# Queries packed two heads to a slot: four slot products per batch in place of six

## The reference, cut to what matters

```python
q = split_heads(tokens @ Wq, HEADS)
kv = split_heads(tokens @ Wkv, HEADS)
k, v = (kv[..., :DK], kv[..., DK:])
q, k, v = (l2norm(q), l2norm(k), l2norm(v))
sim = jnp.einsum('bhid,bhjd->bhij', q, k)
attn = jnp.square(jax.nn.relu(sim))
out = jnp.einsum('bhij,bhjd->bhid', attn, v)
out = tanh_norm(out)
```

## Time and profile before

| | |
|---|---|
| median of 3 runs | 542.15 us (540.87 to 542.36) |
| time of the profiled execution | 541.96 us |
| its span, first to last instruction | 539.8 us |
| outside the span | 2.2 us |
| mean granted clock of TensorE | 0.994 of full speed |
| busy: PE, DVE, ACT, POOL | 96%, 77%, 69%, 65% of the span |

### The profile page before, as it was taken

One profiled execution on the slowest core, in us unless ns is written; L12 is line 12 of the kernel. 1 busy time (PEld: TensorE's weight loads), 2 busy tenths in 40 slices (PEclk: granted clock), 3 DMA queues, 4 the chain that ended last, 5 costly groups with the idle time before them and its releaser, 6 DMA issues.

```text
span 539.8 us, 10360 instructions
## 1 busy us (share of the span) xinstructions
PE 519.2 (96%) x3334; PEld 389.9 (72%) x3334; DVE 417.8 (77%) x1001; ACT 370.3 (69%) x675; POOL 349.7 (65%) x311
## 2 busy tenths in 40 slices
PE   8798999999999999999999999999999999999997
PEld 7566667676766666778787777777778767788884
DVE  6767888889888886688588688598598678786765
ACT  6597878879788965454757945955955955855553
POOL 6756869696977782776568456466566555666562
PEclk9799999999999999999999999999999999999999
DMA  8400000101010001910762921940940850861930
GB/s 219 132 1 2 1 15 18 46 2 46 2 46 14 4 2 64 215 41 5 181 134 77 214 56 43 211 95 27 222 98 18 213 136 6 191 141 54 215 70 19
DMA packets 37269, 44.50 MB, mean 82 GB/s; under 512 B 5856, under 2 KB 20448, under 8 KB 37216
## 3 DMA queue, kind: packets, MB, share of 16 engines
q1 hardware_dynamic: 32528, 42.14, 33.7%
q10 hardware_dynamic: 4688, 1.71, 1.3%
HBM read 40.68 MB, written 3.15 MB: 81 GB/s over the span
## 4 chain that ended last, share of the span: by engine, by line
PE 45%; POOL 30%; issue 18%; DVE 5%; ACT 2%; POOLq 0%; DVEq 0%; ACTq 0%
PE PS L1317 44%; POOL hl L564 14%; POOL vi L458 4%; POOL sr L479 4%; POOL v L475 1%; POOL qs L467 1%; POOL rstd L504 1%; POOL sqq L469 1%; DVE aT L973 1%; POOL mrstd L555 1%; POOL rsA L443 1%; DVE n L944 1%; DVE PS L1186 0%; DVE hb L1191 0%; ACT sqv L612 0%
## 5 line engine op out<-in xcount | busy, mean ns | idle before, releaser
L564 POOL TENSOR_TENSOR hl<-hb,hh 128x512 fp32r<-128x512 f32 x127 | 164.6, 1297 | 128.7 <-ACT hh L792 127.8
L785 ACT ACTIVATE sil<-PS 128x512 f32<-128x512 f32 (+1 forms) x136 | 81.1, 596 | 78.2 <-PE PS L1317 73.1
L1186 DVE TENSOR_TENSOR PS<-sil,PS 128x512 f32<-128x512 f32 x128 | 88.3, 690 | 53.1 <-PE PS L1317 30.7
L1317 PE MATMUL PS<-fxh,wfh 128*128 128x512 f32 x264 | 104.6, 396 | 2.3 <-DVE hb L1191 1.5
L792 ACT ACTIVATE hh<-hb 128x512 fp32r<-128x512 f32 x128 | 80.4, 628 | 38.4 <-DVE hb L1191 37.4
L1317 PE MATMUL PS<-fxh,wfl 128*128 128x512 f32 x264 | 104.2, 395 | 0.0
L1317 PE MATMUL PS<-fxl,wfh 128*128 128x512 f32 x264 | 104.0, 394 | 0.0
L1191 DVE TENSOR_TENSOR hb<-PS,wbc 128x512 f32<-128x512 f32 x128 | 88.5, 691 | 12.3 <-issue 5.4
L973 DVE SCALAR_TENSOR_TENSOR aT<-PS,rl 128x1024 f32<-128x1024 f32 x64 | 75.8, 1218 | 20.3 <-ACT rl L627 20.2
L627 ACT ACTIVATE rl<-PS 128x1024 f32<-128x1024 f32 x64 | 63.8, 1028 | 19.0 <-PE PS L1317 18.9
L1317 PE MATMUL PS<-aT,v 128*64 128x256 f32 x512 | 62.3, 385 | 0.0
(11 more groups left out here) (197 smaller groups left out, 890.1 us busy)
## 6 DMA issues: line engine op xcount, KB each, us to landing
wbc<-w_dram SPq DMA_DIRECT2D x48, 512.0 KB, 11.8
wbc<-w_dram SPq DMA_DIRECT2D x32, 128.0 KB, 3.0
wbc<-w_dram SPq DMA_DIRECT2D x16, 256.0 KB, 4.3
wfs<-wf_dram SPq DMA_DIRECT2D x32, 98.0 KB, 2.1
band_dram<-zero SPq DMA_DIRECT2D x16, 80.0 KB, 1.7
band<-band_dram ACTq DMA_DIRECT2D x4, 320.0 KB, 2.9
Osb<-wa_dram SPq DMA_DIRECT2D x3, 256.0 KB, 3.6
X<-x_dram SPq DMA_DIRECT2D x1, 768.0 KB, 6.7
```

What stands on the lines that cost most here:

```text
L564: g.tensor_tensor(hl[:, n % RING, :], hb[:, n % RING, :], hh[:, n % RING, :].bitcast(F32), ALU.subtract).then_inc(F("hl"), 1)
L785: s.activation(sil[0:rows, n % 2, :], PS[0:rows, G0 + n % 2, :], ACT.Silu).then_inc(F("silu"), 1)
L1186: v_.tensor_tensor(PS[:, bank, :], sil[:, n % 2, :], PS[:, bank, :], ALU.mult).then_inc(F("t"), 1)
L1317: return nc.tensor.matmul(o, w, m, start=start, stop=stop)
```

## The change

The queries are packed like the keys: groups 0 and 1 share a block of 128 weight columns, groups 2 and 3 another. `queries(n)` makes both blocks in one bank with two slot products, `keys(n)` the keys with two more. ACT then reads the bank of the queries twice, each time through `Identity` with a scale that is a column of 0s and 1s per partition (`own`) and a bias that is a column of zeros: the first copy keeps the even groups' rows and sets the others to 0, the second the odd groups'. The bank counts as read only after the second copy; a semaphore `even` marks the first. `own` is made on DVE at the start by four small instructions. The weights are 256 columns fewer, and each group has one turn of a bank less (two per batch for queries and keys in place of three).

```diff
-WQ_G, WK_G = (0, 1, 4, 5), (2, 3)
-W_V = 2 * NQ * P
+EVEN, KEYS, ODD = 0, 1, 2
+W_Q, W_K, W_V = 0, 2 * P, 4 * P
-FIRST_WEIGHTS = (("in_wv0", slice(W_V, W_V + 512)), ("in_wv1", slice(W_V + 512, WA)), ("in_wq0", slice(0, 4 * P)),
-                 ("in_wq1", slice(4 * P, W_V)))
+FIRST_WEIGHTS = (("in_wv0", slice(W_V, W_V + 512)), ("in_wv1", slice(W_V + 512, WA)), ("in_wk", slice(W_K, W_V)),
+                 ("in_wq", slice(W_Q, W_K)))
...
-    order += [("v", 0, t, k) for t in range(2) for k in range(2)] + [("g", 0, j) for j in range(NQ)]
+    order += [("v", 0, t, k) for t in range(2) for k in range(2)] + [("k", 0), ("q", 0)]
...
-        order += coming(n, ("g", n, 0), ("g", n, 2), ("g", n, 1)) + [("nb", n)]
+        order += coming(n, ("q", n), ("k", n)) + [("nb", n)]
...
             def square_queries(n, k):
-                pool.wait_ge(*freed("g", n, 2 * k))
+                pool.wait_ge(*freed("q", n))
                 pool.wait_ge(*full("nb", n - 1))
-                g.tensor_tensor(qs[:, k, :], qk[:, n % 2, 2 * k, 0:L], qk[:, n % 2, 2 * k, L:2 * L], ALU.add).then_inc(A("qs"), 1)
+                g.tensor_tensor(qs[:, k, :], qk[:, n % 2, EVEN, k * L:(k + 1) * L], qk[:, n % 2, ODD, k * L:(k + 1) * L],
+                                ALU.add).then_inc(A("qs"), 1)
...
-            def keep_group(n, j):
-                act.wait_ge(*full("g", n, j))
+            def keep_queries(n, par):
+                act.wait_ge(*full("q", n))
+                if n == 0:
+                    act.wait_ge(cs("own"), 2)
+                    act.wait_ge(cs("zero"), 1)
                 after(act, A("S"), 2 * NG * (n - 1))
-                s.activation(qk[:, n % 2, j, :], PS[:, bank_of("g", n, j), :], ACT.Copy).then_inc(free_of("g", n, j), 1)
+                done = free_of("q", n) if par else A("even")
+                s.activation(qk[:, n % 2, (EVEN, ODD)[par], :], PS[:, bank_of("q", n), :], ACT.Identity, bias=zero[:, 0:1],
+                             scale=own[:, par:par + 1]).then_inc(done, 1)
+
+            def keep_keys(n):
+                act.wait_ge(*full("k", n))
+                after(act, A("S"), 2 * NG * (n - 1))
+                s.activation(qk[:, n % 2, KEYS, :], PS[:, bank_of("k", n), :], ACT.Copy).then_inc(free_of("k", n), 1)
...
-            keep_group(0, 0)
-            keep_group(0, 1)
+            keep_keys(0)
+            keep_queries(0, 0)
             square_values(0, 1)
-            keep_group(0, 2)
+            keep_queries(0, 1)
             relu(0)
...
                 relu_half(NG * b + 1, 0)
                 if more:
-                    keep_group(n, 0)
+                    keep_queries(n, 0)
                 relu_half(NG * b + 1, 1)
...
                 if more:
-                    keep_group(n, 2)
-                    keep_group(n, 1)
+                    keep_queries(n, 1)
+                    keep_keys(n)
                     square_keys(n)
...
             v_.tensor_copy(rowg[:, :], rowh[:, :]).then_inc(cs("rg"), 1)
+            v_.tensor_scalar(rowp[:, :], rowid[:, :], DK, None, ALU.bitwise_and).then_inc(cs("rp"), 1)
+            dve.wait_ge(cs("rp"), 1)
+            v_.tensor_copy(rowq[:, :], rowp[:, :]).then_inc(cs("rq"), 1)
+            dve.wait_ge(cs("rq"), 1)
+            for par in range(2):
+                v_.tensor_scalar(own[:, par:par + 1], rowq[:, 0:1], float(DK * par), None, ALU.is_equal).then_inc(cs("own"), 1)
...
             def first_square_queries(k):
-                dve.wait_ge(*freed("g", 0, 2 * k))
+                dve.wait_ge(*freed("q", 0))
...
-            def group(n, j):
-                bank, done = turn("g", n, j)
+            def slot_wise(n, w0, bank):
                 for part in range(2):
-                    cols = slice((2 * j + part) * P, (2 * j + part + 1) * P)
-                    last = split3(PS[:, bank, part * L:(part + 1) * L], wah[:, cols], wal[:, cols],
-                                  xTh[:, :], xTl[:, :])
-                last.then_inc(done, 1)
+                    cols = slice(w0 + part * P, w0 + (part + 1) * P)
+                    last = split3(PS[:, bank, part * L:(part + 1) * L], wah[:, cols], wal[:, cols], xTh[:, :], xTl[:, :])
+                return last
+
+            def queries(n):
+                bank, done = turn("q", n)
+                slot_wise(n, W_Q, bank).then_inc(done, 1)
+
+            def keys(n):
+                bank, done = turn("k", n)
+                slot_wise(n, W_K, bank).then_inc(done, 1)
+
+            def wait_queries(b, g):
+                if g % 2:
+                    pe.wait_ge(*freed("q", b))
+                else:
+                    pe.wait_ge(A("even"), b + 1)
...
             def score(i):
...
-                jq, q0, k0 = WQ_G[g] // 2, WQ_G[g] % 2 * L, g // 2 * L
-                pe.wait_ge(*freed("g", b, jq))
-                pe.wait_ge(*freed("g", b, 1))
+                jq, c0 = (EVEN, ODD)[g % 2], g // 2 * L
+                wait_queries(b, g)
+                pe.wait_ge(*freed("k", b))
...
                 if more:
                     pe.wait_ge(*freed("xT", n))
-                    for j in (0, 2, 1):
-                        group(n, j)
+                    queries(n)
+                    keys(n)
```

More of the change, by code:

```diff
@@ L183, in hybrid_layer @@
         rowg = sb("rowg", [P, 1])
+        rowp = sb("rowp", [P, 1], I32)
+        rowq = sb("rowq", [P, 1])
+        own = sb("own", [P, 2])
         sel = sb("sel", [P, 2, P], F32R)
@@ L226, in hybrid_layer @@
         Z = Sems(ctx, nc, "full0 full5 full6 full7 free0 free5 free6 free7")
-        ld = Sems(ctx, nc, "in_x0 in_x in_wv0 in_wv1 in_wq0 in_wq1 in_x1 in_wo in_wf0 in_wf1 in_wf2 in_wf3 in_wf4 in_wf5 in_wf6 in_wf7 in_sd in_gw in_wb in_bb zeroed")
-        cs = Sems(ctx, nc, "id0 id half floors rid ind0 indp0 ind indp rm rf rh rg sel fpad zero sel1 sdz wah wal wph wpl wfh wfl sdh sdl")
-        A = Sems(ctx, nc, "stats mv ve rstd xn xTh vraw sqv n2v nv n2o nbo qs sqq sqk rr vi vc0 vc vp S relu a av Oc sqO "
+        ld = Sems(ctx, nc, "in_x0 in_x in_wv0 in_wv1 in_wk in_wq in_x1 in_wo in_wf0 in_wf1 in_wf2 in_wf3 in_wf4 in_wf5 in_wf6 in_wf7 in_sd in_gw in_wb in_bb zeroed")
+        cs = Sems(ctx, nc, "id0 id half floors rid ind0 indp0 ind indp rm rf rh rg rp rq own sel fpad zero sel1 sdz wah wal wph wpl wfh wfl sdh sdl")
+        A = Sems(ctx, nc, "stats mv ve rstd xn xTh vraw sqv n2v nv n2o nbo even qs sqq sqk rr vi vc0 vc vp S relu a av Oc sqO "
                           "sr sr_half n th nmx rec f1 ff fhi f")
@@ L598, in tokens_high @@
                 if n:
-                    act.wait_ge(*full("g", n - 1, NQ - 1))
+                    act.wait_ge(*full("k", n - 1))
                 s.activation(xTh[:, :], PS[:, bank_of("xT", n), 0:L], ACT.Copy).then_inc(A("xTh"), 1)
@@ L612, in square_values @@
                 s.activation(sqv[:, :], v[:, n % 2, t, :], ACT.Square).then_inc(A("sqv"), 1)
[L614 to L617 removed]
+            def keep_queries(n, par):
[3 more added lines that the diff above has]
+                    act.wait_ge(cs("zero"), 1)
+                after(act, A("S"), 2 * NG * (n - 1))
+                done = free_of("q", n) if par else A("even")
[5 more added lines that the diff above has]
+                s.activation(qk[:, n % 2, KEYS, :], PS[:, bank_of("k", n), :], ACT.Copy).then_inc(free_of("k", n), 1)
             def square_keys(n):
[L620 removed]
+                act.wait_ge(*freed("k", n))
                 act.wait_ge(*full("nb", n - 1))
[L622 removed]
+                s.activation(sqk[:, :], qk[:, n % 2, KEYS, :], ACT.Square).then_inc(A("sqk"), 1)
             def relu_half(i, f):
@@ L1366, in score @@
                         rows = slice(SLOT * s, SLOT * (s + 1))
-                        last = mm(PS[:, S0 + s, jt * L:(jt + 1) * L], qk[rows, b % 2, 1, k0 + jt * P:k0 + (jt + 1) * P],
-                                  qk[rows, b % 2, jq, q0:q0 + L], True, True)
+                        last = mm(PS[:, S0 + s, jt * L:(jt + 1) * L], qk[rows, b % 2, KEYS, c0 + jt * P:c0 + (jt + 1) * P],
+                                  qk[rows, b % 2, jq, c0:c0 + L], True, True)
                         if jt == 1 and s % 2 == 1:
@@ L1497, in _ @@
             pe.wait_ge(cs("wpl"), 1)
-            group(0, 0)
-            group(0, 1)
+            keys(0)
             pe.wait_ge(cs("wpl"), 2)
-            group(0, 2)
+            queries(0)
             fill_idle(4, "xT", 1)
@@ L1514, in _ @@
                 if b < 2:
-                    fill_idle(4 if b == 0 else 8, "g", n, 0)
+                    fill_idle(4 if b == 0 else 8, "q", n)
                 if b == 0:
```

14 lines of the change are left out of this document (7 added, 7 removed).

## The result

The kernel with the packed queries takes 551.74 us in the median of 6 runs (549.13 to 554.53), the kernel before 542.07 in the 6 runs beside it: a ratio of 1.0189, 95% interval 1.0153 to 1.0226, slower by 9.7 us. Forecast were 549.8 and a range of 546 to 555. The profiled execution takes 552.22 us, with a span of 550.4 against 539.8.

A forecast was written before the change was run, and what follows sets the result against it. PE looked like the bound (24.40 of 24.50 us a pass), with the chain of ACT copy, POOL squares and `pair_sums` close behind. Start +3.0 and passes +4.85 made +7.85 on 541.96: 549.8 us, range 546 to 555.

The forecast's parts named there:

- the narrow one (546.5 to 552): Whole kernel: the span of times given to the forecast case itself, with chance 0.72.
- PE ready at G + 5.55: Each pass: six matmuls fewer (0.72 us) bring PE to `pair_sums` 5.55 us after the group matmuls start (G).
- The copies, 780 ns: ACT's query copies: two pointer operands add a fixed 176 ns to 604, giving 780 ns.
- the rival of a cost by the element (1308): ACT's query copies: pointer cost grows with elements, 1308 ns a copy, 7.4 us more, 557 us; chance 0.04.
- The wait that appears: POOL's first square waits for ACT's second copy; `pair_sums` (P) starts 7.29 us after the group matmuls (G), losing 1.02 us.
- P to the next G, 18.23: Each pass: from `pair_sums` (P) to the next group matmuls (G) PE runs without a stall, unchanged at 18.23 us.
- The term of -0.41: Pass 1: PE's 0.41 us wait for DVE behind `pair_sums` goes away, leaving net +0.61 of +1.02.
- Pass 0, +1.37: First loop pass: the second copy delays `pair_sums` from 29.38 to 30.75, +1.37 us; PE's saving is hidden.
- the clock falls too: Rival: PE's stands drop the clock; 553 to 556 us for one or two passes, 565 to 568 for six; chance 0.10.
- The start, +3.0: Before the loop: DVE's first square waits 2.49 us for the second copy, and `own` takes 0.5 us.
- PE's saving comes through: Rival: faster, 539.9 us or 536.9 with the start hidden, if the second copy ends by G + 1.6; chance 0.08.
- The stands are partly made up: Rival: part of the waits is given back behind `pair_sums`, 540.6 to 546 us; chance 0.06.

The follow-up runs named there:

- squares from the bank: Changed kernel, but one ACT Square reads the packed queries from PSUM; POOL's and DVE's sums and squares of the queries are gone: 538.40 us, ratio 0.9926.
- Wait alone: Kernel before the change, only the first square of the queries also waits for the copy standing second on ACT: 546.86 us, ratio 1.0093.
- plain copies: Changed kernel, both query copies made without per-partition scale and bias, so no rows are set to zero: 547.48 us, ratio 1.0099.
- the second copy early: Changed kernel, in the loop ACT's second query copy stands ahead of the second half of the relu: 544.26 us, ratio 1.0042.
- own late: Changed kernel, the four DVE instructions making `own` moved behind the low part of batch 0's tokens: 549.79 us, ratio 1.0140.
- the start's copy early: Changed kernel, for batch 0 alone ACT makes the second query copy ahead of the square of the values: 551.65 us, ratio 1.0177.
- the split later: Changed kernel, POOL splits the query and key weights only after DVE has made the low part of batch 0's tokens: 550.18 us, ratio 1.0153.
- the two edits to the start: Changed kernel with ACT squaring the query bank, plus `own` made later and POOL's weight split delayed: 536.42 us, ratio 0.9897.

## Why the prediction was right, and where its sizes were off

The sign held, and so did the mechanism of the passes: POOL's squares wait for ACT's second copy, and PE for the squares. The time is 1.9 us above the 549.8 and inside both ranges, but the narrow one (546.5 to 552) is met by 0.3 us and by luck. In the profiled execution the start, passes 0 and 1 and small rests add up to 3.8 us more than the working has; 1.08 us less in the expert stage and 0.3 us less outside the span, neither of them in the working, take some of it back. The case that came is the forecast with part of a rival in it: the clock fell twice, for 3.1 us. One of the prediction's own signs of being wrong, a clock of 0.5 within the loop, is there too, in pass 0. Point by point:

- *PE ready at G + 5.55.* Shown with the squares from the bank, where nothing else holds P: G + 5.55, and a pass shorter by 0.73 us (forecast 0.72).
- *The copies, 780 ns.* 777 measured. The fixed cost was the right reading, and the rival of a cost by the element (1308) falls. The Trainium skill, "ScalarE: Activation LUTs", section "What ACT_TABLE_LOAD costs", gives about 93 ns for each of the two pointers; the trace agrees, with 87.
- *The wait that appears.* P at G + 7.29 forecast, 7.28 measured; the stand 1.7 and 1.66; the pass 25.5 and 25.50. Wait alone, plain copies and the second copy early move the pass to 25.14, 25.14 and 24.59, and each time P stands where the end of the second copy and POOL's 3.8 us put it.
- *P to the next G, 18.23.* 18.22 in passes 2 to 4. In pass 1 it was to get shorter by the 0.41 us for which PE waited for DVE; it took 17.73 for 17.77. The term of -0.41 was wrong. The wait is still there, 0.29 us for 0.41, and PE's next wait for DVE has grown by about as much (0.93 for 0.84); that the stand moves ACT and DVE along with PE is my reading of it, which no run shows. In pass 5 the change was -0.12 for -0.23, in pass 6 +0.13 for +0.04.
- *Pass 0, +1.37.* At P, +1.14. But the stand there is 2.1 us, not 1.7, for the same reason as in the working: PE's matmuls there are fewer and P no earlier. Behind it the clock fell, +1.53. I had this as a rival for the passes at large, and held it unlikely by the 1.41 us stand of the earlier trace rows that did no harm; the pass with the longest stand needed a price of its own. So the rival "the clock falls too" came true in one pass of seven, at half of the 3.0 that I gave it, and once more in the start.
- *The start, +3.0.* This is the term most out: +5.01 in the profiled execution. The wait itself was right (2.57 for 2.49), and `own` cost 0.28 for 0.5. The step that failed is "The smaller load and POOL's splitting of 256 columns less are hidden behind the value products ...; without that cover they could only gain": the smaller piece is there earlier (POOL takes it up between 5.33 and 6.15 in the kernels that have it and an unchanged split, at 6.10 and 6.47 in the two that have the larger), POOL works beside DVE, and DVE is what PE waits for (0.69 us in this execution). The value products at 1.2 GHz add 1.58 (8.19 to 12.63 is 4.44 us, 7.22 to 10.08 was 2.86). With the 0.28 of `own` that is 2.55 us at the first slot product, in the place of the 0.5 that I had. The second copy then ends 0.25 us earlier than 2.55 and the 2.49 of the working would put it, and DVE's work behind the square adds 0.22.
- *PE's saving comes through*, the rival on the other side, failed by its own condition: the second copy was over at G + 3.35, not by 1.6. When the condition is taken away (squares from the bank), it comes true, at 0.9926.
- *The stands are partly made up.* Not behind `pair_sums`: P to the next G has not got shorter by more than the 0.04 us of pass 1. The 1.08 us in the expert stage lie within what that stage differs by between traces.

What stays open: why the clock falls in pass 0 behind a 2.1 us stand in three profiled executions (the kernel after, own late, the start's copy early) and not in a fourth (the split later); why it falls in pass 2 with three kernels (plain copies, the start's copy early, the squares from the bank) and in no pass beyond 0 in the kernel after; and whether the value products run slow in most executions. With plain copies and with the second copy early they start late as well (8.10 and 8.93, behind stands of 1.19 and 1.39 us), and take 2.89 and 2.85 us, the full clock; with the squares from the bank they take 5.10 us, behind a stand of 0.73 us. So neither the late start nor the length of the stand decides it, and the 1.58 us may be of some executions and not of others. No run was made for it.

## What to carry to other kernels

When a dense engine meets a chain that ends just ahead of it, take the distance first: here the chain of copy, square and sum ended 0.77 us ahead of PE's arrival, and a change that moved one link by 1.75 us lost 1.0 us a pass, while the 0.72 us taken off the busiest engine came to nothing until that chain was cut. Where two consumers read one product, ask whether one of them can read the source itself: squaring the bank directly made the same packing 0.7% faster than the kernel before instead of 1.9% slower, and 1.0% faster with the two edits to the start. And a load made smaller can land earlier, so look for what then starts beside it.

## What was unexpected of the hardware

DVE and POOL hold each other up here when both read two SBUF operands, and which of them pays goes with who starts first. The scaling of the values shows it. DVE and POOL before:

```profile
19.71 1.22 DVE L1099 TENSOR_TENSOR v<-v,vc 128x1024 f32<-128x1024 f32 x1
...
19.73 2.96 POOL L475 TENSOR_TENSOR v<-v,vc 128x1024 f32<-128x1024 f32 x1
```

and after:

```profile
24.73 1.90 POOL L479 TENSOR_TENSOR v<-v,vc 128x1024 f32<-128x1024 f32 x1
24.93 2.78 DVE L1119 TENSOR_TENSOR v<-v,vc 128x1024 f32<-128x1024 f32 x1 [0.25 <-DVE vc L1115]
```

The first to start takes 1.22 us (DVE) or 1.90 us (POOL, its usual time for this tile), and the other stretches: the two instructions together last until 22.69, 2.98 us after the first start, and until 27.71, also 2.98. An order that costs nothing in sum can thus take 1.06 us off POOL and put 1.56 us on DVE. POOL's cast, which reads one operand, stretches as well: in the start's second copy early it took 1.22 us beside DVE's pair and 0.40 us without it, while the pair kept its 1.29 us.

And the clock: it fell behind the stand of 2.1 us in pass 0 of the kernel after, with own late and with the start's second copy early, but with the split later it stayed at 2.4 GHz behind a stand just as long (2.08 us; P to the next G 15.90), as it did behind those of 1.66 to 1.78 us in passes 1 to 5 of the kernel after. So the length of the stand alone doesn't decide it. With spare products in the stand it stayed up.
